# A mixture-of-experts layer's second product in three rounded parts, split by three engines slot by slot

## What is computed

```
h = relu(einsum('te,td,edf->tf', onehot, xn, W1) + b1[idx])     # D = 256 -> F = 1024
y = einsum('te,tf,efd->td', onehot, h, W2) + b2[idx]             # F = 1024 -> D = 256
x = x + tanh(g_ffn[1]) * y * gates                               # one expert idx per token
```

## Time and profile before

| | |
|---|---|
| device time, 3 runs | 878.24 us median (876.4 to 881.36) |
| span of the profiled execution, first to last instruction | 875.4 us |
| what that execution took in all | not listed apart; the lowest run is 1.0 us above its span |
| TensorE busy in the span | 802.4 us, 92% |
| VectorE, ScalarE, GpSimd busy | 546.3 (62%), 366.9 (42%), 373.1 us (43%) |
| mean granted TensorE clock | 0.950 of 2.4 GHz |
| slots' share of the chain that ended last | L2105 9%, L2093 9% |

### The profile page before, as it was taken

How to read it: one execution, slowest core, us unless ns; L and a number is a source line. 1 busy time by engine, 2 the same in 40 slices (tenths; PEclk the granted TensorE clock), 3 DMA queues, 4 the chain that set the end, 5 groups by cost and what they waited for, 6 DMA issues and landing times.

```text
span 875.4 us, 13801 instructions
## 1 busy us (share of the span) xinstructions
PE 802.4 (92%) x4270; PEld 612.4 (70%) x4271; DVE 546.3 (62%) x1173; ACT 366.9 (42%) x1175; POOL 373.1 (43%) x396
## 2 busy tenths in 40 slices
PE   6888799999999899989999999999998799999995
PEld 4555445555555555548888878888886689999994
DVE  4958765777677756675998667777766433333331
ACT  4457133544354332344444366776660032222220
POOL 7256553344447364345475044444442312222221
PEclk9999599989899988999999999999998799999998
DMA  8580000000000000003600093000001364555520
GB/s 303 170 307 35 1 0 1 1 1 0 1 1 1 0 1 1 0 1 111 255 1 0 1 301 104 12 19 13 14 12 61 101 266 176 182 180 176 174 80 3
DMA packets 31887, 67.14 MB, mean 77 GB/s; under 512 B 3103, under 2 KB 22909, under 8 KB 30813
## 3 DMA queue, kind: packets, MB, share of 16 engines
q1 hardware_dynamic: 28699, 56.17, 18.3%
q0 software_dynamic: 2560, 10.17, 3.6%
q10 hardware_dynamic: 578, 0.19, 0.1%
HBM read 54.74 MB, written 12.68 MB: 77 GB/s over the span
## 4 chain that ended last, share of the span: by engine, by line
PE 67%; DVE 17%; issue 6%; ACT 3%; POOL 3%; DMA 2%; DVEq 0%; SPq 0%; ACTq 0%; POOLq 0%
PE PS L2105 9%; PE PS L2093 9%; PE PS L1488 7%; PE PS L734 6%; PE PS L1468 6%; PE PS L1296 5%; PE PS L1274 3%; PE PS L725 3%; PE PS L771 3%; PE PS L701 3%; PE PS L726 2%; DVE row_best L846 2%; PE PS L743 2%; POOL rrms L551 2%; ACT pc L1670 1%
## 5 line engine op out<-in xcount | busy, mean ns | idle before, releaser
L1055 ACT ACTIVATE EX<-PS 128x512 f32<-128x512 f32 x144 | 78.9, 594 | 133.4 <-PE PS L726 130.6
L846 DVE TENSOR_REDUCE row_best<-PS 128x1 f32<-128x1024 f32 x64 | 77.8, 1221 | 41.8 <-PE PS L701 41.5
L1015 POOL TENSOR_TENSOR sumP<-sumP,EX 128x1024 f32<-128x1024 f32 x32 | 75.7, 2364 | 43.1 <-ACT EX L1055 42.7
L1670 ACT ACTIVATE pc<-PS,mx 128x77 f32<-128x77 f32 x256 | 78.8, 359 | 26.8 <-DVE mx L1565 26.8
L2093 PEld LDWEIGHTS PS<-xeT,w 128*128 128x128 f32 x736 | 85.6, 192 | 3.6 <-DMA w<-in_L_ffn_W 1.3
L2093 PE MATMUL PS<-xeT,w 128*128 128x128 f32 x736 | 86.1, 275 | 2.0 <-DMA w<-in_L_ffn_W 1.1
L2105 PE MATMUL PS<-w,heT 128*128 x368 | 83.3, 379 | 1.3 <-DVE oe L2035 1.3
L2132 POOL DMA_INDIRECT out<-oe,target x23 | 23.2, 1011 | 126.1 <-DVE oe L2035 126.1
L734 PE MATMUL PS<-EX,V 128*64 128x512 f32 (+1 forms) x288 | 76.5, 640 | 0.0
L2105 PEld LDWEIGHTS PS<-w,heT 128*128 128x128 f32 x368 | 68.1, 190 | 10.0 <-issue 1.7
L1488 PE MATMUL PS<-vw,pcT 128*128 128x256 f32 (+1 forms) x320 | 73.0, 383 | 1.2 <-ACT pcT L1683 1.2
(11 more groups left out here) (283 smaller groups left out, 1716.1 us busy)
## 6 DMA issues: line engine op xcount, KB each, us to landing
w<-in_L_ffn_W SPq DMA_DIRECT2D x31, 1024.0 KB, 10.1
vw_rows<-vwn SPq DMA_DIRECT2D x2, 1232.0 KB
kwH_rows<-kwH SPq DMA_DIRECT2D x1, 2464.0 KB, 7.4
kwL_rows<-kwL SPq DMA_DIRECT2D x1, 2464.0 KB, 13.7
kwH<-kwH_rows POOLq DMA_DIRECT2D x1, 2464.0 KB, 12.3
kwL<-kwL_rows POOLq DMA_DIRECT2D x1, 2464.0 KB, 19.2
vw<-vw_rows SPq DMA_DIRECT2D x2, 1152.0 KB, 13.3
XR<-in_x SPq DMA_DIRECT2D x4, 512.0 KB, 13.4
```

Source lines behind the costliest of these rows:

```text
L846: dve.tensor_reduce(row_best[:, n % 2, t // GT, t % GT:t % GT + 1], PSf[:, 512 * at:512 * at + S], AX.X, ALU.max, negate=True).then_inc(ma ...
L1015: pool.tensor_tensor(sumP[:], before, EX[:, (KT * n + c) % EB, :, :], ALU.add).then_inc(pool_summed, 1)
L1055: act.activation(EX[0:r, k % EB, i, :], PS[0:r, ST_AT + i, :], ACT.Exp).then_inc(exp_done, 1)
L1670: last = act.activation(pc[:, p, h * C:h * C + C], PS[:, 1 + part, (h - h0) * C:(h - h0) * C + C], ACT.Exp, bias=mx1[:, p, h:h + 1], accum ...
```

## The change

Down becomes three products of type float32r, one pass each: high rows by high weights, high rows by low weights, low rows by high weights, 24 instructions where 16 stood. "High" is a value rounded to float32r, "low" the rest. The splitting is done for each slot:

- ScalarE, *high_weights*(n + 2): a copy of the slot's 2048 elements of `w2` into `wd` high, once down(n) is done.
- VectorE, *low_weights*(n + 2): `w2` less `wd` high, first half (1024 elements), behind finish(n).
- GpSimd, *low_weights*(n + 2): the second half, behind send(n) and gather(n + 4).
- GpSimd, *high_rows*(n + 1): a rounding copy of all 1024 elements of the rows `heF`, once both activates are done, ahead of send(n).
- VectorE, *low_rows*(n + 1): `heF` less `heH`, in place, behind its own activate(n + 1) and ahead of finish(n).

Down(n) waits for finish(n - 1) as before, then for the high rows and weights, the low weights, and the low rows, each ahead of its part. Several semaphores of the routing are merged into common ones with the same order; ScalarE now waits for the routing's table and for all of `w2` and `b2` ahead of its first copy, since `wd` lies where the routing's one-hot tables were.

```diff
+    heH = Region(CROSS_LOW).take("heH", [P, 2, FC, P], F32R)
+    wd = Region(MIDDLE + 4 * KC * F).take("wd", [P, 2, 2, FC * D], F32R)
...
+    heF = Region(moe.at).take("heF", [P, 2, FC, P])
+    heL = moe.take("heL", [P, 2, FC, P], F32R)
...
+        def low_rows(n, p):
+            dve.wait_ge(he_high, n + 1)
+            dve.tensor_tensor(heL[:, p, :, :], heF[:, p, :, :], heH[:, p, :, :].bitcast(F32), ALU.subtract).then_inc(he_low, 1)
+        def low_weights(n, p):
+            e = dve.value_load(expert_of[0:1, ds(n, 1)], min_val=0, max_val=E - 1)
+            dve.wait_ge(wd_high, n + 1)
+            dve.tensor_tensor(wd[:, p, 1, 0:HALF], w2f[:, ds(e * (FC * D), HALF)], wd[:, p, 0, 0:HALF].bitcast(F32),
+                              ALU.subtract).then_inc(wd_low_dve, 1)
...
+                low_rows(n + 1, 1 - u % 2)
             finish(n, u)
-        dve.wait_ge(expert_ready, 1)
-        dve.wait_ge(b2_in, 16)
+            if after:
+                low_weights(n + 2, u % 2)
...
+        def high_weights(n, p):
+            e = act.value_load(expert_of[0:1, ds(n, 1)], min_val=0, max_val=E - 1)
+            if not isinstance(n, int) or n > 1:
+                act.wait_ge(g2_done, n)
+            act.activation(wd[:, p, 0, :], w2f[:, ds(e * (FC * D), FC * D)], ACT.Copy).then_inc(wd_high, 1)
...
+                high_weights(n + 2, u % 2)
+        act.wait_ge(slots_listed, EXPERTS)
+        act.wait_ge(routed_by_pe, TABLE)
+        act.wait_ge(w2_in, 16 * E + 16)
+        high_weights(0, 0)
         affine(0, 0)
+        high_weights(1, 1)
...
-            e = pe.value_load(expert_of[0:1, ds(n, 1)], min_val=0, max_val=E - 1)
             pe.wait_ge(oe_ready, n + 4)
-            pe.wait_ge(heT_act, n + 1)
-            pe.wait_ge(heT_dve, n + 1)
-            w = w2[:].rearrange("p e c d -> p (e c d)")
+            pe.wait_ge(he_high, n + 1)
+            pe.wait_ge(wd_high, n + 1)
             for c in range(FC):
-                last = pe.matmul(PS[:, 5 + p, 0:D], heT[:, p, c, :], w[:, ds(e * (FC * D) + c * D, D)], start=c == 0,
-                                 stop=c == FC - 1)
+                pe.matmul(PS[:, 5 + p, 0:D], heH[:, p, c, :], wd[:, p, 0, c * D:c * D + D], start=c == 0, stop=False)
+            pe.wait_ge(wd_low_dve, n + 1)
+            pe.wait_ge(wd_low_pool, n + 1)
+            for c in range(FC):
+                pe.matmul(PS[:, 5 + p, 0:D], heH[:, p, c, :], wd[:, p, 1, c * D:c * D + D], start=False, stop=False)
+            pe.wait_ge(he_low, n + 1)
+            for c in range(FC):
+                last = pe.matmul(PS[:, 5 + p, 0:D], heL[:, p, c, :], wd[:, p, 0, c * D:c * D + D], start=False, stop=c == FC - 1)
...
+        def high_rows(n):
+            pool.wait_ge(heT_act, n + 1)
+            pool.wait_ge(heT_dve, n + 1)
+            pool.tensor_copy(heH[:, n % 2, :, :], heF[:, n % 2, :, :]).then_inc(he_high, 1)
+        def low_weights(n):
+            e = pool.value_load(expert_of[0:1, n:n + 1], min_val=0, max_val=E - 1)
+            pool.wait_ge(wd_high, n + 1)
+            pool.tensor_tensor(wd[:, n % 2, 1, HALF:], w2f[:, ds(e * (FC * D) + HALF, HALF)],
+                               wd[:, n % 2, 0, HALF:].bitcast(F32), ALU.subtract).then_inc(wd_low_pool, 1)
         pool.wait_ge(rows_out, 16 * NT)
-        pool.wait_ge(source_ready, 1)
+        pool.wait_ge(slots_listed, SOURCES)
         for n in range(4):
             gather(n)
-        pool.wait_ge(source_ready, 2)
+        pool.wait_ge(slots_listed, TARGETS)
+        low_weights(0)
+        low_weights(1)
+        high_rows(0)
         for n in range(SLOTS):
+            if n + 1 < SLOTS:
+                high_rows(n + 1)
             send(n)
             if n + 4 < SLOTS:
                 gather(n + 4)
+            if n + 2 < SLOTS:
+                low_weights(n + 2)
```

More of the change, by code:

```diff
@@ L302, in layers_kernel @@
     placed = moe.take("placed", [P, NT, SLOTS, 4])
+    heH = Region(CROSS_LOW).take("heH", [P, 2, FC, P], F32R)
+    wd = Region(MIDDLE + 4 * KC * F).take("wd", [P, 2, 2, FC * D], F32R)
+    assert MIDDLE + 4 * KC * F + 4 * FC * D <= TOP and CROSS_LOW + 2 * FC * P <= MIDDLE
     moe = Region(TOP)
@@ L354, in layers_kernel @@
          "x3_ready x3_copied x3T_done x3T_ready lg_done lg_ready x3_stats x3_meanvar x3_var x3_once")
[L356 to L362, removed]
+    (routed_by_pe, oh_ready, gexp_ready, slots_onehot, placed_half, slots_listed) = sems(
+         "routed_by_pe oh_ready gexp_ready slots_onehot placed_half slots_listed")
+    WR_SUMMED, RANKED, TABLE = 1, 2, 3
+    EXPERTS, SOURCES, TARGETS = 1, 2, 3
+    HIGH_ONEHOT, LOW_ONEHOT = 1, 2
+    (e_z, e_zT, e_zT_ready, g1_done, heT_act, heT_dve, e_biased, g2_done, oe_ready, he_high, he_low, wd_high,
+     wd_low_dve, wd_low_pool) = sems(
+         "e_z e_zT e_zT_ready g1_done heT_act heT_dve e_biased g2_done oe_ready he_high he_low wd_high "
+         "wd_low_dve wd_low_pool")
     bank_free = [sem(f"bank_free{k}") for k in range(3)]
@@ L1812, in pe_route @@
             last = pe.matmul(PS[:, 2, 0:E], onesq[:], wr[:, k, :], start=k == 0, stop=k == KC - 1)
-        last.then_inc(wr_summed, 1)
+        last.then_inc(routed_by_pe, 1)
         keep_busy(pe, 8)
@@ L1816, in pe_route @@
         pe.matmul(PS[:, 0, 0:NT * E], upper[:], flat(RT[:, 1]), start=True, stop=True)
-        pe.matmul(PS[:, 1, 0:NT * E], onesq[:], flat(RT[:, 1]), start=True, stop=True).then_inc(rank_done, 1)
+        pe.matmul(PS[:, 1, 0:NT * E], onesq[:], flat(RT[:, 1]), start=True, stop=True).then_inc(routed_by_pe, 1)
         keep_busy(pe, 12)
         for half in range(2):
-            pe.wait_ge(low_half, 1 + half)
+            pe.wait_ge(slots_onehot, LOW_ONEHOT + half)
             pe.wait_ge(placed_half, 1 + half)
@@ L1824, in pe_route @@
                                  start=n == 0, stop=n == NT - 1)
-        last.then_inc(table_done, 1)
+        last.then_inc(routed_by_pe, 1)
         keep_busy(pe, 10)
@@ L1940, in dve_route @@
         dve.tensor_scalar(expert_of[:], top[:, 0:4, :].rearrange("p a b -> p (a b)")[:, 0:SLOTS], float(E - 1), None,
-                          ALU.min).then_inc(expert_ready, 1)
-        dve.wait_ge(table_done, 1)
+                          ALU.min).then_inc(slots_listed, 1)
+        dve.wait_ge(routed_by_pe, TABLE)
         rows = PS[:, 3, 0:SLOTS * 4].rearrange("p (s f) -> p s f", f=4)
-        dve.tensor_scalar(source[:], rows[:, :, TOKEN], -1.0, 0.0, ALU.add, ALU.max).then_inc(source_ready, 1)
+        dve.tensor_scalar(source[:], rows[:, :, TOKEN], -1.0, 0.0, ALU.add, ALU.max).then_inc(slots_listed, 1)
         own.add(dve.tensor_copy(table[:].rearrange("p s f -> p (s f)"), PS[:, 3, 0:SLOTS * 4]))
@@ L1991, in load @@
             load_up(n, u)
-        sp.wait_ge(expert_ready, 1)
+        sp.wait_ge(slots_listed, EXPERTS)
         load_up(0, 0)
@@ L2003, in sp_experts @@
             load(n, n % 4)
+    HALF = FC * D // 2
+    w2f = w2[:].rearrange("p e c d -> p (e c d)")
     of_buffer = lambda n, u: 4 * n + (16 - 4 * u)
@@ L2042, in body @@
                 activate(n + 1, 1 - u % 2)
+                low_rows(n + 1, 1 - u % 2)
             finish(n, u)
-        dve.wait_ge(expert_ready, 1)
-        dve.wait_ge(b2_in, 16)
+            if after:
+                low_weights(n + 2, u % 2)
+        dve.wait_ge(slots_listed, EXPERTS)
+        dve.wait_ge(w2_in, 16 * E + 16)
+        low_weights(0, 0)
         norm(0, 0)
         norm(1, 1)
+        low_weights(1, 1)
         activate(0, 0)
+        low_rows(0, 0)
         slot_tiles(dve, body)
@@ L2115, in body @@
             down(n, p)
-        pe.wait_ge(expert_ready, 1)
+        pe.wait_ge(slots_listed, EXPERTS)
         turn(0, 0)
```

25 lines of the change are left out of this document (11 added, 14 removed).

## The result

The changed kernel takes 923.38 us (median of 4 runs, 920.63 to 928.73) where the kernel before took 878.66 in the same series (4 runs, 876.4 to 881.36): a ratio of 1.051, 95% interval 1.047 to 1.056. Slower was forecast, at 921.5 us. The profiled execution spans 918.9 us, against 918.7 in the working.

A forecast was written before the change was run, and what follows sets the result against it. The prediction took the chain from finish to finish through GpSimd and VectorE as the bound: 9.45 us a slot against 7.25, +43.3 on the 875.4 span, 918.7, plus 2.84 to the median, 921.5 us; range 905 to 945.

The forecast's parts named there:

- The relay through GpSimd and VectorE: Slot loop: finish, send, gather, low_weights, high_rows, low_rows, next finish run in a chain without overlap, 9.45 us a slot.
- finish to the gather's end: Slot loop, VectorE's finish, then GpSimd's send and gather: 4.17 us, taken from the timeline before the change.
- register load: GpSimd loads the expert's number between gather and subtraction: 0.40 us, the middle of 0.07 and 0.73.
- subtraction: GpSimd's low_weights, its half of the weights, 1024 elements, inside the chain: 2.36 us.
- rounding, with its hand-over: GpSimd's high_rows behind its low_weights: 1.04 us for 1024 elements and 0.07 hand-over, 1.11 together.
- low_rows, with its hand-over: VectorE's low_rows after GpSimd's high_rows: 0.09 us hand-over and 1.22 for the subtraction, 1.31 together.
- low_rows' end to finish: VectorE, from low_rows to the next finish: 0.10 us, its register load possibly done while it subtracts.
- The last step: End of the loop, finish(21) to finish(22): 5.01 us before, 0.64 less with one shorter down.
- The clock: Rival: gaps of 2.84 us a slot keep TensorE at half clock, 13.2 us a slot, 1009 us; chance 0.04.
- the gap ahead of turn: TensorE idles 2.84 us a slot, in one piece ahead of its turn, waiting on the loop.
- GpSimd is slowed: Rival: VectorE's work meets GpSimd's subtraction and lengthens it, +1.01 us a round, 943 us, range 930 to 960; chance 0.13.
- TensorE keeps the pace: Rival: rounds under TensorE's 6.61 us let its 0.64 a slot come through, 864 us; chance 0.06 for the faster case.

The follow-up runs named there:

- rows on ScalarE: Against the changed kernel, ScalarE instead of GpSimd makes the rounding copy of the rows, and GpSimd keeps its subtraction: 904.2 us, ratio 1.030.
- norm early: Against the kernel with finish ahead of low_rows, norm runs one slot earlier, ahead of VectorE's low_weights: 876.26 us, ratio 0.998.
- the last kernel: Against the kernel with norm one slot earlier, VectorE also does GpSimd's half of the weights' subtraction: 867.5 us, ratio to before 0.989.

## Why the prediction held, step by step

**What bounds it.** The relay through GpSimd and VectorE was forecast and is there, piece by piece. Breaking its queue order at one line (finish ahead of low_rows) takes 923 to 879 with all the work in place, so it was the order and not the amount of work.

**The terms.** The sum was right to 0.01 us, and that is partly luck, since its errors cancel:

| piece of the round | priced | measured |
|---|---|---|
| finish to the gather's end | 4.17 | 4.87 |
| register load | 0.40 | 0.02 |
| subtraction | 2.36 | 2.40 |
| rounding, with its hand-over | 1.11 | 0.97 |
| low_rows, with its hand-over | 1.31 | 1.26 |
| low_rows' end to finish | 0.10 | -0.08 |
| sum | 9.45 | 9.44 |

- *The mis-sized term is "finish to the end of the gather".* The prediction took it from the earlier trace rows and wrote that while VectorE subtracts, GpSimd waits or issues a transfer, so the lone durations hold. The order is as it said, but issuing a transfer isn't independent of VectorE: send takes 1.71 instead of 1.01 beside VectorE's low_weights. The kernel without VectorE's half gives that 0.70 back. The working also let norm run beside GpSimd's subtraction at its lone length; here they don't meet (norm ends at 768.06, the subtraction starts at 769.92), and where they do, norm takes 2.43.
- *The register load.* Between 0.07 and 0.73 it was set at 0.40. The subtraction starts 0.02 after the gather ends (769.90 to 769.92), so the load hides. In the chain of waits GpSimd's queue has it at 767.48, while send runs: the engine's queue works ahead of the engine.
- *Hand-overs.* The rounding begins 0.08 before the subtraction's record ends, and finish before low_rows' does, where 0.07 and 0.10 were added.

**The bounds around the loop.** 19 rounds: 179.0 (708.70 to 887.71), priced 179.6. Two without a gather: 16.0, priced 16.3. The first finish came 1.4 earlier, at 708.70, where no move was forecast. The last step took 6.71 (903.74 to 910.45), not 4.37: behind a gap of 4.21 TensorE ran its 24 products at clock 0.51, 1.2 of 2.4 GHz, in the stretch shown above. Together 43.5 on the span, 43.3 forecast.

**The clock.** Clock 0.84 in the stretch around 770 us stems from pieces at half the rate, such as 777.50 to 780.50 (mean 0.51). The round at 777 isn't longer for it: finishes stay 9.43 to 9.44 apart, since down has slack. It cost time only at the very end. It also shows in the gap ahead of turn, forecast near 2.8: 2.57 behind up at full clock, in the row at 777.55, but 2.0 in the mean (37.8 us in 19 waits), since a slot with such a piece keeps TensorE busy longer.

**The rivals.** *GpSimd is slowed* didn't come about as named: while GpSimd subtracts, VectorE waits, and the subtraction takes 2.40, priced 2.36. What was slowed on GpSimd is send, by 0.70 a round. In the kernels where the two subtractions do meet, in the loop VectorE's waits and GpSimd's stays near 2.40. But GpSimd is slowed where VectorE comes first: by 0.04 us at the start of the slots (3.39, rows on ScalarE), and in the spiking layer before the change, where the square behind the 395.07 of the earlier trace rows starts 0.23 later and takes 1.36 instead of 1.04. *TensorE keeps the pace* was rightly judged unlikely in this order; the working's next chain behind it (ScalarE's copy, VectorE's half, norm, turn, down, 7.4) is what the kernel with finish first ran into, at 7.22. Two more changes opened that, and 867.5 is near the 864 the rival named.

**Where the experiments' theories failed.** Twice the time saved by a reordering was overrated because of the hold: with the rounding ahead on GpSimd's queue at most 1.5 us were allowed for the meeting, against 2.17 measured (3.39 less 1.22), and with the rounding on ScalarE nothing. A third time, with norm early, the theory counted no hold, and its rival only that of the subtractions, but the second half of finish, which also reads two operands in SBUF, is held too.

## What to carry to other kernels

When work is split over VectorE and GpSimd, write down the closed chain of waits and queue neighbours of one round and add it up before adding up busy time: here no engine was more than 82% busy (TensorE, 16.38 of 20) and a line's place was worth 45 us. Then mark VectorE's instructions with two operands in SBUF, and those like norm (from SBUF to SBUF), and on GpSimd the subtractions, rounding copies and issues of indirect transfers. Where two marked ones, one of each engine, overlapped in time here, one of them mostly waited, without a semaphore. Giving GpSimd half of a subtraction took 2.40 us there, while VectorE does all 2048 elements in 2.28.

## What the hardware showed that was not expected

- VectorE is held by GpSimd, in full and not in part. Low_rows, 1.22 alone, ends 1.09 after GpSimd's subtraction whether it came 2.30 or 1.74 us before that end. A rounding copy with a single input holds VectorE too (finish's second half 0.98 instead of 0.48, ending 0.28 after the copy). GpSimd's own hardly move in these loops: 2.38 to 2.42 for the subtraction and 1.04 to 1.06 for the copy in the rows shown here.
- GpSimd is held as well where VectorE comes first: its subtraction took 3.39 behind one of VectorE's that started 0.04 us earlier (696.82, rows on ScalarE). A start 0.67 us earlier didn't protect VectorE in one other round (848.60, norm early: 4.18 instead of 1.22), so who comes first isn't the whole rule, and the rest stays open.
- What is held has two operands in SBUF, or is norm (one operand in SBUF, 2.43 instead of 0.41). Activate and the first half of finish, which read PSUM, kept their 1.11 and 0.42 beside the same subtraction (857.47 and 858.70 in the kernel with norm early).
- An indirect transfer's issue on GpSimd that starts while a subtraction of VectorE runs ends some 0.8 to 0.9 us after it: send 768.62 behind 767.74, the gather in the last kernel 780.66 behind 779.82. One that starts at the same moment or earlier isn't lengthened: send 1.03 at 710.67, the gather 0.97 at 784.63. Which part of the issue waits, no run here shows.
